# Dense layers of a graph network: last biases added by VectorE from a tile on all lanes, node rows stored chunk by chunk

## The chip, the cores and the metric

One core of one Trainium2 chip runs the kernel in one launch. The metric is the device time of that launch in microseconds (us), a median over runs; the profile is one more execution, recorded by the hardware profiler. PE is the matmul engine, PEld its weight loads, DVE VectorE, ACT ScalarE, POOL GpSimd, SP the engine whose queue issues most of the plain DMAs.

## The reference, cut to what matters

Four graph layers run one after the other on 6250 nodes of 32 features and 100,000 edges. Between the sums over edges, every node goes through small dense layers. Those that the change touches are:

```python
h = relu(h @ W1a + b1a);  h = relu(h @ W2a + b2a)     # 32 -> 64 -> 64, first half of layer 0 ("B" below)
h = relu(h @ W1b + b1b);  x = x + (h @ W2b + b2b)     # 64 -> 64 -> 32, second half ("C")
feat_src = h @ W2s + b2s; feat_dst = h @ W2d + b2d    # 32 -> 64 and 32 -> 64, layer 1 ("D")
x = x + ((feat + g_sum) @ W1 + b1)                    # 32 -> 32, end of layer 1 ("E")
t = elu(h @ stn3_w + stn3_b) @ stn4_w + stn4_b        # 64 -> 64 -> 3, layer 3 ("F")
```

A sixth product, 125 -> 64 without a bias ("A"), forms the first spline layer. The results of B (as three bf16 parts of each float, 192 values a node) and the source half of D (64 floats a node) are written to a table in device memory, `node_rows`, from which the next phase gathers a row for each edge.

## The kernel before, in words

The 6250 nodes lie as 49 blocks of 128: block j holds node 128 j + p on partition (lane) p. The program is a chain of phases. `phase` opens semaphores and buffers, the engines run their own instruction lists in it, and it ends with a clearing of its semaphores (line 78) and a barrier of all engines (L79), so nothing of a phase runs before the one ahead has ended.

`dense_phase` (L1076) makes all six products. It walks over 13 chunks: twelve of four blocks and a last one of one block. For a chunk, TensorE turns the blocks (L1142), ScalarE copies them out of PSUM (L1186), TensorE forms the hidden layer if there is one (L1157), ScalarE adds its bias and applies relu (L1198; for elu it is VectorE at L1219, L1220 and L1227 with ScalarE's exp at L1190), TensorE forms the last layer back in node order (L1168), and VectorE takes it out of PSUM with a `finish` function: `copy_to` (L1249), `over_zero_to` (L1270) or `add_to` (L1277). The stages are one chunk apart (`lags`): in one step, TensorE first makes the last layer of an older chunk, then the hidden layer of the next, then turns a third. Every PSUM and stage buffer is double; the semaphores `copied`, `made`, `back` and `taken` count chunks, and each engine waits for the counts in the order in which its list has them.

The last layer's bias lies in a tile of one partition, four times over. Before the products of L1168, TensorE multiplies a row of ones (cleared to 1.0 by VectorE at L1204) with it, which writes the bias to all 128 lanes of the PSUM bank (L1164); the products then add to it. This product stands behind the same waits (`copied`, `taken`) as the products of L1168.

Weights and biases are loaded by SP at the start of each dense phase, behind VectorE's clearing of the weight tiles (L1055, then L1062 for weights, L1068 for the last layer's bias and L1072 for a bias over partitions). The first product of a phase waits for all these loads.

In B, a `behind` function (L1260 to L1264) splits what was taken into three bf16 parts after each chunk. After B, and again after D, `store_nodes_phase` (L1028) writes the table in a phase of its own: one DMA of all 49 blocks (L1035), and a wait for it.

Of the kernel before, what the change touches and what calls it, by code (L numbers as in the profile page):

```python
# [7 lines left out]
BF16 = mybir.dt.bfloat16  # L8
# [1016 lines left out]

def store_nodes_phase(k, table, src):  # L1028
    nc = k.nc
    with phase(nc) as ph:  # L1030
        stored = ph.sem("stored")
        with nc.Block() as block:
            @block.sync
            def _(sp):
                sp.dma_start(table.rearrange("(j p) f -> p j f", p=LO), src).then_inc(stored, 16)  # L1035
                sp.wait_ge(stored, 16)


class Layer:


# [3 lines left out]
    def hold(self, k, ph, K, blocks, onwards):  # L1045


        self.K, self.blocks, self.onwards, self.ways = K, blocks, onwards, blocks // onwards
        self.weight = sb(k, ph, "weight", [blocks * K, self.ways, onwards * self.C])
        across_nodes = self.end is not None  # L1050
        self.bias = sb(k, ph, "bias", [onwards * self.C, 1] if across_nodes else [1, 4, self.C]) if self.biases else None
        self.loads = blocks * len(self.weights) + len(self.biases) * (onwards if across_nodes else 1)

    def clear(self, dve):
# [2 lines left out]
    def load(self, eng, sem):  # L1057
        for n in range(self.blocks):
            col = n % self.onwards * self.C
            for of in self.weights:  # L1060
                to = self.weight[n * self.K:(n + 1) * self.K, n // self.onwards, col:col + of.shape[1]]
                eng.dma_start(to, of).then_inc(sem, 16)  # L1062
                col += of.shape[1]
        col = 0
        for of in self.biases:
            width = of.shape[0]
            if self.end is None:
                eng.dma_start(self.bias[:, :, col:col + width], across(of, 4).unsqueeze(0)).then_inc(sem, 16)  # L1068
# [7 lines left out]
def dense_phase(k, src, K, layers, finish, behind=None):  # L1076

# [19 lines left out]
    with phase(nc) as ph:  # L1097
        for n, layer in enumerate(layers):
# [7 lines left out]
        ones = sb(k, ph, "ones", [1, LO])  # L1106
        turned, back, taken, own, cleared, weighed, ready = ph.sems("turned", "back", "taken", "own", "cleared", "weighed", "ready")
        copied = [ph.sem(f"copied{s}") for s in range(S + 1)]
        made = [ph.sem(f"made{s}") for s in range(S)]
        lowered = [ph.sem(f"lowered{s}") for s in range(S)]  # L1110
# [8 lines left out]
        with nc.Block() as block:  # L1119
            @block.sync  # L1120
            def _(sp):
                sp.wait_ge(cleared, S + 1)
                for layer in layers:
                    layer.load(sp, weighed)

            @block.tensor
            def _(pe):
                for step in range(len(chunks) + lags[-1]):
                    for s in range(S + 1, -1, -1):
# [30 lines left out]
                        else:  # L1160
                            if n >= 2:
                                pe.wait_ge(taken, n - 1)
                            if layer.bias is not None:
                                nc.tensor.matmul(out_p[b][:, 0:count, :].rearrange("p j f -> p (j f)"), ones[:],  # L1164
                                                 layer.bias[:, 0:count, :].rearrange("p j f -> p (j f)"), start=True, stop=False)
                            for q, blocks in stacks(S, count):
                                at = q // packs[S] * LO
                                m = nc.tensor.matmul(out_p[b][:, q:q + blocks, :].rearrange("p j f -> p (j f)"),  # L1168
                                                     of[0:blocks * layer.K, at:at + LO], layer.weight[0:blocks * layer.K, 0, 0:blocks * C_out],
                                                     start=layer.bias is None, stop=layer.bias is None or q + blocks == count)  # L1170
                            m.then_inc(back, 1)

            @block.scalar
# [27 lines left out]
            @block.vector  # L1201
            def _(dve):
                c = Chain(dve, own)
                dve.memset(ones[:], 1.0)  # L1204
                for layer in layers:
                    layer.clear(dve).then_inc(cleared, 1)

# [21 lines left out]
                for step in range(len(chunks) + 2):  # L1229
                    for s in range(1, S + 1):  # L1230
                        if elus[s - 1]:
                            if step < len(chunks):
                                raised(s, step)
                            if 0 <= step - 1 < len(chunks):
                                joined(s, step - 1)
                    n = step - 2
                    if n < 0:
                        continue
                    first, count = chunks[n]
                    dve.wait_ge(back, n + 1)  # L1240
                    finish(dve, out_p[n % 2][:, 0:count, :], first, count).then_inc(taken, 1)
                    if behind is not None:
                        dve.wait_ge(taken, n + 1)
                        behind(dve, c, first, count)


def copy_to(dest):
    def finish(dve, made, first, count):
        return dve.tensor_copy(dest[:, first:first + count, :], made)  # L1249
    return finish  # L1250


# [13 lines left out]


def over_zero_to(dest):
    def finish(dve, made, first, count):
        return dve.tensor_scalar(dest[:, first:first + count, :], made, 0.0, None, ALU.max)  # L1270
    return finish


def add_to(dest):
    def finish(dve, made, first, count):
# [1430 lines left out]
def gin_layers(k, s_rows, d_rows, making):  # L2706
    nc, w, n, xs = k.nc, k.w, k.dense_w, k.xs
    with layer(k):
        b = sb(k, None, "b", [LO, NB, D_HID])
        with layer(k):  # L2710
# [3 lines left out]
            with layer(k):  # L2714
# [6 lines left out]
                def keep(dve, c, ph):  # L2721
# [3 lines left out]
            first_sum_phase(k, d_rows, y)  # L2725
            add_phase(k, y, h)
            b16 = sb(k, None, "b16", [LO, NB, 3 * D_HID], BF16)
            dense_phase(k, y, D_IN, [Layer([n["W1a"]], [n["b1a"]], D_HID, "relu"), Layer([n["W2a"]], [n["b2a"]], D_HID)],
                        over_zero_to(b), split_to(k, b, D_HID, b16))
            table = dram(k, "node_rows", [NN, 3 * D_HID], BF16)  # L2730
            store_nodes_phase(k, table, b16[:])
        a = sb(k, None, "a", [LO, NB, D_HID])
        with layer(k):
            second_sum_phase(k, table, a, making)
# [5 lines left out]
def attention_layer(k, d_rows, lists, conv, shift):  # L2740
    n, xs = k.dense_w, k.xs
    with layer(k):
# [10 lines left out]
        with layer(k):  # L2753
            a.tops, a.sums = late("tops"), late("sums")
            with layer(k):
                feat = sb(k, None, "feat", [LO, NB, 2 * D_HID])
                dense_phase(k, h, D_IN, [Layer([n["W2s"], n["W2d"]], [n["b2s"], n["b2d"]], 2 * D_HID)], copy_to(feat))
                store_nodes_phase(k, table, feat[:, :, 0:D_HID])
# [130 lines left out]
```

## Time and profile before

| | |
|---|---|
| time, median of 3 runs | 11930.78 us (11922.58 to 11940.91) |
| profiled execution: span from first to last instruction | 11956.6 us |
| PE / DVE / POOL / ACT busy, share of the span | 49% / 53% / 52% / 28% |
| granted TensorE clock, mean of the span | 0.578 |
| dense phases with the stores behind them (A, B, C, D, E, F) | about 2871 to 2917, 3165 to 3234, 4808 to 4858, 4870 to 4945, 8420 to 8451, 8469 to 8525 us |

The profiled execution has no time of its own beside its span; the span is 25.8 us (0.2%) longer than the median of the three timed runs. In a timeline row the first two numbers are the start and the length in us, then engine, line, operation, output and input names, partitions and elements, and how many instructions the row merges; a bracket gives the idle time before it and what ended it. Names with digits are shown without them (`in_L_gnn_b2a_dram` is an input). A matrix product of 4-byte floats appears as two instructions.

### The profile page before, as it was taken

The page shows a single profiled execution, that of the slowest core. Times are in us where ns is not written, and L with a number is a line of the kernel's source. Part 1 is how long each engine was busy: PE and PEld are TensorE (multiplying, and loading weights), DVE is VectorE, ACT ScalarE, POOL GpSimd, SP SyncE. Part 2 cuts the span into 40 slices and gives each one's busy share as a digit, 9 for nine tenths or more (in the row PEclk, how much of TensorE's full clock was granted, in tenths as well). Part 3 has the DMA queues.
Part 4 walks back from the last instruction along what each step waited for, and adds up shares of the span by engine and source line. Part 5 has one row for each costly group of instructions (what it writes and reads, how often), then busy time and mean ns, then how long its engine had stood idle before and what let it go on. Part 6 is the DMA issues. An engine that isn't in the chain of part 4 may idle for free. (4 is left out here: it accounts for less than half of the span.)

```text
span 11956.6 us, 144077 instructions
## 1 busy us (share of the span) xinstructions
PE 5851.1 (49%) x32456; PEld 4649.4 (39%) x32585; DVE 6365.8 (53%) x16741; ACT 3375.5 (28%) x7561; POOL 6265.8 (52%) x8257
## 2 busy tenths in 40 slices
PE   4223244434566566566666466666433333742222
PEld 2111133333444344355555466666333333422222
DVE  6444555554311111366666788888455555654555
ACT  0000022222133333111111477777312111321111
POOL 3767566663155555255555344444055565046665
PEclk8555565655566666565656555555655555865555
DMA  6331222222555555122223699999111112876666
GB/s 192 111 110 57 60 56 58 58 57 66 169 190 190 183 190 175 34 67 67 67 66 66 262 350 349 350 350 351 73 38 38 38 38 37 296 256 199 194 199 180
DMA packets 894565, 1760.03 MB, mean 147 GB/s; under 512 B 486979, under 2 KB 487288, under 8 KB 889897
## 3 DMA queue, kind: packets, MB, share of 16 engines
q0 software_dynamic: 317952, 1023.05, 27.3%
q1 hardware_dynamic: 537384, 598.27, 15.0%
q10 hardware_dynamic: 39168, 138.04, 2.9%
q8 instruction: 23, 0.38, 0.0%
q14 instruction: 38, 0.30, 0.0%
HBM read 1150.36 MB, written 611.50 MB: 147 GB/s over the span
## 5 line engine op out<-in xcount | busy, mean ns | idle before, releaser
L1764 POOL DMA_INDIRECT got<-corners,now x1664 | 1599.6, 961 | 1835.4 <-issue 1064.2
L1764 POOL DMA_INDIRECT got<-node_rows,now x1664 | 1602.6, 963 | 1713.3 <-issue 1334.6
L1764 POOL DMA_INDIRECT got<-patches,now x832 | 795.8, 956 | 899.5 <-issue 603.1
L948 POOL DMA_INDIRECT d_rows<-row x832 | 836.0, 1005 | 533.7 <-issue 522.6
L1670 PE MATMUL made_p<-weights,turned 64*128 64x320 f32 x2450 | 795.4, 648 | 559.2 <-ACT z L1694 295.4
L2567 PE MATMUL sum_p<-msg_s,hot_s 128*128 128x64 f32 x3328 | 737.3, 423 | 595.4 <-DVE msg_s L2022 595.4
L699 POOL DMA_INDIRECT s_rows<-row_now,pos_i x784 | 756.6, 965 | 379.5 <-issue 372.0
L2567 PEld LDWEIGHTS sum_p<-msg_s,hot_s 128*128 128x128 f32 x3328 | 717.7, 332 | 604.3 <-DVE msg_s L2022 604.3
L2106 PE MATMUL acc_p<-msg,hot_s 128*128 128x32 f32 x1664 | 376.2, 402 | 1004.5 <-DVE msg L2030 785.1
L1812 DVE TENSOR_TENSOR a<-a,sum_p 128x64 f32 x832 | 183.5, 221 | 1244.0 <-remote 785.5
L1694 ACT COPY z<-made_p 128x384 f32<-128x384 f32 x1225 | 526.4, 489 | 973.0 <-DMA d_rows<-row 516.7
L1670 PEld LDWEIGHTS made_p<-weights,turned 64*128 64x128 f32 x2450 | 457.7, 262 | 830.5 <-ACT z L1694 407.8
L2106 PEld LDWEIGHTS acc_p<-msg,hot_s 128*128 128x128 f32 x1664 | 362.7, 330 | 1018.8 <-issue 1018.8
L155 POOL MEMSET spare<- 128x192 f32 x2472 | 694.1, 281 | 0.9
L268 DVE TENSOR_TENSOR hot<-column,lo_s 128x1024 bf16<-128x1024 bf16 x312 | 215.2, 690 | 673.9 <-DMA got<-node_rows,now 645.2
L2016 DVE TENSOR_TENSOR got<-got,weight 128x512 f32<-128x512 f32 x832 | 518.7, 684 | 58.3 <-PE sum_p L2567 19.5
L2092 ACT CAST hot_s<-hot 128x1024 f32<-128x1024 bf16 x104 | 212.4, 2042 | 1148.1 <-DVE hot L268 898.8
L886 DVE TENSOR_TENSOR sums<-sums,sum_p 128x126 f32 x832 | 237.9, 286 | 557.6 <-DMA d_rows<-empty 320.0
L2681 ACT ACTIVATE prod<-prod,below,alpha 128x32 f32<-128x32 f32 x1664 | 516.4, 398 | 0.0
L912 PE MATMUL feat_p<-h,turned_s 128*128 x832 | 122.1, 264 | 770.3 <-ACT turned_s L926 694.5
L632 PE MATMUL rank_p<-one,before 128*128 128x400 bf16 x98 | 48.8, 498 | 858.2 <-DVE one L417 697.2
L1961 ACT COPY turned_s<-turned_p 128x1024 bf16<-128x1024 bf16 x104 | 105.3, 1012 | 1265.1 <-remote 717.2
(424 smaller groups left out, 15148.1 us busy)
## 6 DMA issues: line engine op xcount, KB each, us to landing
corners<-z SPq DMA_DIRECT2D x245, 960.0 KB
corners<-z SPq DMA_DIRECT2D x98, 864.0 KB
d_rows<-empty ACTq DMA_DIRECT2D x32, 1586.0 KB
row<-d_rows SPq DMA_DIRECT2D x104, 488.0 KB
corners<-z SPq DMA_DIRECT2D x49, 672.0 KB
s_rows<-empty ACTq DMA_DIRECT2D x32, 962.0 KB
row<-s_rows SPq DMA_DIRECT2D x104, 296.0 KB
got<-node_rows,now POOLq DMA_INDIRECT x1664
```

What stands on the lines that cost most here:

```text
L155: pool.memset(self.of[:, t, :], 0.0).then_inc(self.cleared, 1)
L268: return dve.tensor_tensor(out, column16, mid(lo, LO), ALU.is_equal)
L699: pool.indirect_dma_start(out=s_rows, out_offset=bass.IndirectOffsetOnAxis(ap=pos_i[b][:, t, 0:1], axis=0), in_=row_now[b][:, t, :], in_of ...
L886: c.after(dve.tensor_tensor(to, to, part(1 - b2, t), ALU.add))
L948: pool.indirect_dma_start(out=d_rows, out_offset=bass.IndirectOffsetOnAxis(ap=to[:, t, DPOS:DPOS + 1], axis=0), in_=row[b][:, t, :], in_of ...
L1670: nc.tensor.matmul(self.made_p[s % self.BANKS][:, 0:self.col], self.turned[rows, :], self.weights[rows, q * self.col:(q + 1) * self.col], ...
L1694: self.k.nc.scalar.copy(to, of).then_inc(self.out, 1)
L1764: pool.indirect_dma_start(out=to[b][:, t, :], out_offset=None, in_=table, in_offset=bass.IndirectOffsetOnAxis(ap=indices.now[b][:, t:t + 1 ...
L2016: m = dve.tensor_tensor(v, v, last(weights[:, now, 2 * n:2 * n + 2], C), ALU.mult)
L2106: m = nc.tensor.matmul(at_block(acc, now[t]), hot_s[b2][:, t, :], msg[b2][:, t, :], start=False, stop=False)
L2567: m = nc.tensor.matmul(sum_p[b2][:, t, :], hot_s[b2][:, t, :], msg_s[b2][:, n, t, :], start=n == 0, stop=n == 1)
L2681: m = nc.scalar.activation(at[:, n, :], at[:, n, :], ACT.Exp, bias=below[b2][:, n:n + 1], scale=alpha[b2][:, n:n + 1])
```

## The change

The bias tile of a last layer becomes 128 partitions by C, loaded by SP from device memory with the same C values for every partition. TensorE's product with the ones is gone, and so are the ones and their clearing. The `finish` functions get the bias as an operand, repeated over the blocks of the chunk: `copy_to` adds instead of copying (a plain copy stays where there is no bias), `over_zero_to` adds out of PSUM and then takes the maximum with zero in SBUF, `add_to` adds the bias to the destination and then the product, in two instructions. VectorE waits for the loads once per phase and counts a few semaphores more per chunk. The store phases are gone: SP, behind its loads, waits for each chunk to be finished by VectorE and stores its rows, and waits for all stores at its end. Three more semaphores belong to each dense phase.

```diff
-def store_nodes_phase(k, table, src):
-                sp.dma_start(table.rearrange("(j p) f -> p j f", p=LO), src).then_inc(stored, 16)
-                sp.wait_ge(stored, 16)
...
-        self.bias = sb(k, ph, "bias", [onwards * self.C, 1] if across_nodes else [1, 4, self.C]) if self.biases else None
+        self.bias = sb(k, ph, "bias", [onwards * self.C, 1] if across_nodes else [LO, self.C]) if self.biases else None
...
-                eng.dma_start(self.bias[:, :, col:col + width], across(of, 4).unsqueeze(0)).then_inc(sem, 16)
+                eng.dma_start(self.bias[:, col:col + width], across(of)).then_inc(sem, 16)
...
+                if shelf is not None:
+                    table, of = shelf
+                    rows = table.rearrange("(j p) f -> p j f", p=LO)
+                    for n, (first, count) in enumerate(chunks):
+                        sp.wait_ge(shelved, n + 1)
+                        sp.sem_inc(storing, 1)
+                        sp.dma_start(rows[:, first:first + count, :], of[:, first:first + count, :]).then_inc(stored, 16)
+                    sp.wait_ge(stored, 16 * len(chunks))
...
-                            if layer.bias is not None:
-                                nc.tensor.matmul(out_p[b][:, 0:count, :].rearrange("p j f -> p (j f)"), ones[:],
-                                                 layer.bias[:, 0:count, :].rearrange("p j f -> p (j f)"), start=True, stop=False)
...
-                                                     start=layer.bias is None, stop=layer.bias is None or q + blocks == count)
+                                                     start=True, stop=True)
...
-                dve.memset(ones[:], 1.0)
...
+                    if n == 0:
+                        dve.wait_ge(weighed, held)
+                        dve.sem_inc(ready, 1)
                     dve.wait_ge(back, n + 1)
-                    finish(dve, out_p[n % 2][:, 0:count, :], first, count).then_inc(taken, 1)
+                    dve.sem_inc(ready, 1)
+                    added = None if bias is None else mid(bias[:], count)
+                    finish(dve, c, out_p[n % 2][:, 0:count, :], added, first, count).then_inc(taken, 1)
+                    if behind is not None or shelf is not None:
+                        dve.wait_ge(taken, n + 1)
+                        dve.sem_inc(ready, 1)
                     if behind is not None:
-                        dve.wait_ge(taken, n + 1)
                         behind(dve, c, first, count)
+                    if shelf is not None:
+                        dve.sem_inc(shelved, 1)
...
 def over_zero_to(dest):
+    def finish(dve, c, made, bias, first, count):
+        to = dest[:, first:first + count, :]
+        c.after(dve.tensor_tensor(to, made, bias, ALU.add))
+        return dve.tensor_scalar(to, to, 0.0, None, ALU.max)
...
 def add_to(dest):
+    def finish(dve, c, made, bias, first, count):
         to = dest[:, first:first + count, :]
+        c.after(dve.tensor_tensor(to, to, bias, ALU.add))
         return dve.tensor_tensor(to, to, made, ALU.add)
```

`c.after` lets VectorE wait until the instruction has finished.

## Rows read from the trace of the kernel before

**Rows 1.** Windows: bounds, us, busy of PE, PEld, DVE, ACT, POOL, clock, DMA, GB/s

```profile
2870.00:2917.00 47.00, 36.29 (x147) 32.32 (x147) 5.57 (x15) 7.30 (x13) 0.00 (x0) 0.50 0.01 1
4877.00:4935.00 58.00, 52.61 (x64) 15.58 (x64) 8.59 (x13) 3.18 (x12) 0.00 (x0) 0.50 0.00 0
3300.00:4800.00 1500.00, 936.78 (x4856) 606.60 (x4856) 264.95 (x1032) 518.01 (x1219) 861.34 (x1187) 0.67 0.54 184
```

**Rows 2.** Timeline of B: one step of the products, and the next one's begin

```profile
3211.61 1.22 PE L1164 MATMUL out_p<-bias,ones 1*128 1x256 f32 x2 [0.35 <-ACT stage L1198]
3212.75 1.22 PE L1168 MATMUL out_p<-weight,stage 128*128 128x128 f32 x4
...
3214.86 0.47 ACT L1198 ACTIVATE stage<-made_p,bias 128x256 f32<-128x256 f32 x1 [3.16 <-PE made_p L1157]
3215.39 1.22 PE L1164 MATMUL out_p<-bias,ones 1*128 1x256 f32 x2 [0.35 <-ACT stage L1198]
```

**Rows 3.** Timeline of B: VectorE's last two chunks, without a pause between them

```profile
3217.87 0.42 DVE L1270 TENSOR_SCALAR b<-out_p 128x256 f32<-128x256 f32 x1 [1.46 <-PE out_p L1168]
3218.33 0.29 DVE L1260 CAST b<-b 128x256 bf16<-128x256 f32 x1
3218.66 0.43 DVE L1261 TENSOR_TENSOR rest<-b,b 128x256 f32<-128x256 f32 x1
...
3220.23 0.23 DVE L1270 TENSOR_SCALAR b<-out_p 128x64 f32<-128x64 f32 x1
...
3221.47 0.19 DVE L1264 CAST b<-rest 128x64 bf16<-128x64 f32 x1
```

**Rows 4.** The store after B: timeline, and SP's waits (us in total, times, longest)

```profile
3222.62 0.40 SPq L1035 DMA_DIRECT2D node_rows<-b  x1
SPq L1032 <- DMA node_rows<-b: 10.3, 1, 10.3
3234.16 0.34 SPq L1626 DMA_DIRECT2D weights<-wide_w  x1
```

**Rows 5.** Timeline of C: the product with the ones and what follows it

```profile
4819.89 0.79 PE L1164 MATMUL out_p<-bias,ones 1*128 1x128 f32 x2
4820.61 0.69 PE L1168 MATMUL out_p<-weight,stage 128*128 128x64 f32 x2
```

**Rows 6.** Timeline of D: one chunk, and the next one's first product

```profile
4882.21 2.07 PE L1164 MATMUL out_p<-bias,ones 1*128 1x512 f32 x2 [0.36 <-ACT stage L1186]
4884.20 2.08 PE L1168 MATMUL out_p<-weight,stage 128*128 128x512 f32 x2
...
4886.85 1.21 PE L1164 MATMUL out_p<-bias,ones 1*128 1x512 f32 x1 [0.35 <-ACT stage L1186]
```

**Rows 7.** The store after D: timeline and SP's waits

```profile
4934.49 0.29 DVE L1249 COPY feat<-out_p 128x128 f32<-128x128 f32 x1 [1.08 <-PE out_p L1168]
SPq L1032 <- DMA node_rows<-feat: 8.4, 1, 8.4
4945.48 0.13 PEld L2324 LDWEIGHTS spread_p<-zero 128*128 128x128 bf16 x2 [11.32 <-issue]
```

**Rows 8.** Timeline of F: the product with the ones and what follows it

```profile
8484.22 0.60 PE L1164 MATMUL out_p<-bias,ones 1*128 1x12 f32 x2 [0.87 <-DVE stage L1227]
8484.75 0.59 PE L1168 MATMUL out_p<-weight,stage 128*128 128x6 f32 x2
```

**Rows 9.** Timeline: clearing, loads of biases (B's, then constants), a store of 106 partitions

```profile
8420.26 0.17 DVE L1204 MEMSET ones<- 1x128 f32 x1 [0.95 <-PEq L79]
...
3170.01 0.69 SPq L1068 DMA_DIRECT2D bias<-in_L_gnn_b2a_dram  x1
3171.98 0.55 PE L1157 MATMUL made_p<-stage,weight 128*128 128x128 f32 x1 [6.47 <-DMA bias<-in_L_gnn_b2a_dram]
...
0.76 0.43 SPq L305 DMA_DIRECT2D attn<-in_L_gnn_attn_dram  x1
...
11948.85 5.11 SPq L2862 DMA_DIRECT2D out_dram<-xs  x1
```

More of the change, by code:

```diff
@@ L1023, in _ @@
                 close_sums(k, acc_p, 7).then_inc(summed, 1)
-def store_nodes_phase(k, table, src):
[L1029 to L1034, printed above, removed]
-                sp.dma_start(table.rearrange("(j p) f -> p j f", p=LO), src).then_inc(stored, 16)
-                sp.wait_ge(stored, 16)
 class Layer:
@@ L1073, in load, with dense_phase @@
             col += width
-def dense_phase(k, src, K, layers, finish, behind=None):
+def dense_phase(k, src, K, layers, finish, behind=None, shelf=None):
     nc = k.nc
@@ L1105, in dense_phase @@
                 for s in range(S)]
-        ones = sb(k, ph, "ones", [1, LO])
         turned, back, taken, own, cleared, weighed, ready = ph.sems("turned", "back", "taken", "own", "cleared", "weighed", "ready")
+        shelved, stored, storing = ph.sems("shelved", "stored", "storing")
         copied = [ph.sem(f"copied{s}") for s in range(S + 1)]
@@ L1203, in _ @@
                 c = Chain(dve, own)
-                dve.memset(ones[:], 1.0)
+                bias = layers[S].bias
                 for layer in layers:
@@ L1239, in _ @@
                     first, count = chunks[n]
+                    if n == 0:
+                        dve.wait_ge(weighed, held)
+                        dve.sem_inc(ready, 1)
                     dve.wait_ge(back, n + 1)
-                    finish(dve, out_p[n % 2][:, 0:count, :], first, count).then_inc(taken, 1)
+                    dve.sem_inc(ready, 1)
[4 more added lines that the diff above has]
+                        dve.sem_inc(ready, 1)
                     if behind is not None:
-                        dve.wait_ge(taken, n + 1)
                         behind(dve, c, first, count)
+                    if shelf is not None:
+                        dve.sem_inc(shelved, 1)
 def copy_to(dest):
-    def finish(dve, made, first, count):
-        return dve.tensor_copy(dest[:, first:first + count, :], made)
+    def finish(dve, c, made, bias, first, count):
+        to = dest[:, first:first + count, :]
+        return dve.tensor_copy(to, made) if bias is None else dve.tensor_tensor(to, made, bias, ALU.add)
     return finish
@@ L1268, in over_zero_to, with finish @@
 def over_zero_to(dest):
-    def finish(dve, made, first, count):
-        return dve.tensor_scalar(dest[:, first:first + count, :], made, 0.0, None, ALU.max)
+    def finish(dve, c, made, bias, first, count):
+        to = dest[:, first:first + count, :]
+        c.after(dve.tensor_tensor(to, made, bias, ALU.add))
+        return dve.tensor_scalar(to, to, 0.0, None, ALU.max)
     return finish
 def add_to(dest):
-    def finish(dve, made, first, count):
+    def finish(dve, c, made, bias, first, count):
         to = dest[:, first:first + count, :]
+        c.after(dve.tensor_tensor(to, to, bias, ALU.add))
         return dve.tensor_tensor(to, to, made, ALU.add)
@@ L2727, in gin_layers @@
             b16 = sb(k, None, "b16", [LO, NB, 3 * D_HID], BF16)
+            table = dram(k, "node_rows", [NN, 3 * D_HID], BF16)
             dense_phase(k, y, D_IN, [Layer([n["W1a"]], [n["b1a"]], D_HID, "relu"), Layer([n["W2a"]], [n["b2a"]], D_HID)],
-                        over_zero_to(b), split_to(k, b, D_HID, b16))
-            table = dram(k, "node_rows", [NN, 3 * D_HID], BF16)
-            store_nodes_phase(k, table, b16[:])
+                        over_zero_to(b), split_to(k, b, D_HID, b16), (table, b16))
         a = sb(k, None, "a", [LO, NB, D_HID])
@@ L2756, in attention_layer @@
                 feat = sb(k, None, "feat", [LO, NB, 2 * D_HID])
-                dense_phase(k, h, D_IN, [Layer([n["W2s"], n["W2d"]], [n["b2s"], n["b2d"]], 2 * D_HID)], copy_to(feat))
-                store_nodes_phase(k, table, feat[:, :, 0:D_HID])
+                dense_phase(k, h, D_IN, [Layer([n["W2s"], n["W2d"]], [n["b2s"], n["b2d"]], 2 * D_HID)], copy_to(feat),
+                            shelf=(table, feat[:, :, 0:D_HID]))
                 score_phase(k, table, feat, d_rows, a)
```

## The prediction, made before the changed kernel was run

> **What bounds the kernel now.** No engine does: on the page's first part PE, DVE and POOL are each busy for about half of the span. The program is a chain of phases with a barrier behind each, so what counts is the length of each phase, and the change touches some 340 us of 11956.6. I therefore read busy time by windows first, then the timeline inside each dense phase, then SP's waits. The windows show two things [rows 1]: in D, TensorE is busy for 52.61 of 58.00 us while VectorE is at 8.59 and ScalarE at 3.18, so TensorE sets D; and the granted clock there is 0.50, that is 1.2 GHz, as it is in A.
>
> The timeline of B [rows 2] shows the circle that sets a step: the product with the ones starts only when ScalarE's relu (0.47 us) has ended, the last layer's products follow, then the hidden layer's, then relu again. 3215.39 - 3211.61 = 3.78 us a chunk, of which 3212.75 - 3211.61 = 1.14 us lie between the start of the product with the ones and the start of the real ones. That product stands behind the wait for relu, so it is on the circle and not beside it. VectorE has 1.46 us of idle time a chunk in B [rows 3], waiting for PE. After the dense work, DMA alone is at work: SP waits 10.3 us for B's store and 8.4 us for D's, and all other engines stand at the barrier [rows 4, 7].
>
> **The products with the ones.** I take the distance of starts, not the length, since consecutive instructions overlap at their ends. It counts for twelve full chunks and once less for the last one of a single block.
> - C: 4820.61 - 4819.89 = 0.72 us [rows 5]; the last chunk has 32 columns, between F's 12 and C's 128, so between 0.53 and 0.72, nearer to the first: 12 x 0.72 + 0.55 = 9.2.
> - D: 4884.20 - 4882.21 = 1.99 us [rows 6]; the last chunk has 128 columns, as C: 12 x 1.99 + 0.72 = 24.6. D's step is 4886.85 - 4882.21 = 4.64 us and becomes 2.65; VectorE's 13 copies take 8.59 us in all [rows 1], 0.66 each, and an add that reads one more operand, were it even twice as long, stays hidden under it.
> - E has the same product of 128 columns as C: 9.2 again.
> - F: 8484.75 - 8484.22 = 0.53 us [rows 8]; 13 x 0.53 = 6.9. Its circle is VectorE's elu, then PE, and an add of 12 elements replaces a copy of 12.
> - C and E have one more VectorE instruction a chunk. It is hidden (a two-operand instruction of 256 elements takes 0.43 [rows 3], these have 128) except in the last chunk, where it delays the end by about 0.2 us and a handover of 0.04 (below): -0.5 in all.
> - A has no bias and gains nothing here.
>
> In **B** the gain is not the whole 1.14 us, because VectorE takes over as the bound. Without the product, PE's circle is 3.78 - 1.14 = 2.64 us. VectorE's six instructions take 3220.23 - 3217.87 = 2.36 us when nothing holds them [rows 3]. The seventh is the maximum with zero in SBUF. No row has it; the nearest are the cast of 256 elements in SBUF (0.29) and the two-operand instruction (0.43). I take 0.29, since it too has one input, plus 0.04 for the handover that the rows show between two chained ones: 2.69. The three semaphore counts more a chunk have no row on VectorE; below, they cost nothing, above, 0.1 us each, more than twice a whole handover. I take 0.02 each: 2.75 us a chunk, between 2.69 and 3.13 (0.43 for the maximum, 0.1 for each count). Before, VectorE takes twelve full chunks in 11 x 3.78 + 2.36 = 43.9 us; after, in 12 x 2.75 = 33.0. Its first take comes 1.14 us earlier, and the last chunk's small seventh instruction and counts add 0.19 + 0.04 + 0.06: 43.9 - 33.0 + 1.14 - 0.29 = 11.8 us. With 3.13 a chunk it is 7.2.
>
> **The stores.** B's last VectorE instruction ends at 3221.66 and the next phase begins at 3234.16 [rows 3, 4]: 12.5 us of tail, made of 0.96 to the issue, 0.40 of issue, 10.3 of waiting and 0.84 of barrier. In the new kernel twelve of thirteen chunks are written while later ones are computed: 10.3 us for 49 blocks make 0.84 us for a chunk of four, and 0.40 to issue it, against a step of 2.75. What stays is the last store. The nearest row for a short DMA from issue to release is the bias load, 3171.98 - 3170.01 = 1.97 us [rows 9]. So the tail is 0.05 + 1.97 + 0.84 = 2.9 us, and the gain 9.6. D's tail is 4945.48 - 4934.78 = 10.7 us [rows 7]; 10.7 - 2.9 = 7.8 gained; a chunk there is 8.4 x 4/49 = 0.7 us of transfer under a step of 2.65. SP has nothing else queued behind its loads, so its new waits hold up no other transfer.
>
> The Trainium skill, "DMA: Bandwidth & Descriptors", sections "Anatomy of one DMA" and "Bandwidth", speaks against this part: each DMA has a fixed cost of about 2.0 us, most of it the receipt of the last write, and one should batch to 1 MiB, where a chunk here has 512 rows of 384 bytes, 192 KB. By its fit a chunk of B would take 2.0 + 0.45 us if no two overlapped, an estimate from that page, still under the step; the last one's 2.1 us would show, and the gain of the two tails would be 0.3 us less in sum. No run here shows a store of this size.
>
> **Small edits.** The clearing of the ones (0.17 us) goes from in front of the weights' clearing in six phases, and SP's loads and PE's start wait for that: 6 x 0.14 = 0.9. The six bias loads (two in D) go to 128 partitions. Issuing one took 0.69 in B; a load of the same kind, 64 floats to 128 partitions, took 0.43 [rows 9]. It moves 128 runs instead of four, so it may land later; I take zero in sum, with 0.26 us less and 0.3 more as bounds for each, so 1.8 us either way. VectorE's new wait for the loads is passed before PE's first product. Three more semaphores a phase are cleared behind the barrier; I put them at 0.2 us in all.
>
> **Sum**: 9.2 + 24.6 + 9.2 + 6.9 - 0.5 + 11.8 + 9.6 + 7.8 + 0.9 - 0.2 = 79.3 us. From the profiled span that is 11956.6 - 79.3 = 11877.3; the span is 25.8 us above the median of the timed runs, and the difference is carried over: 11930.8 - 79.3 = 11851.5, or 0.66% faster.
>
> **The rivals.**
> 1. *The products were hidden anyway.* If the distance of starts were weight loading or waiting that stays, only the stores and clearings gain: 9.6 + 7.8 + 0.9 - 0.2 = 18 us, 11913. For it: PE waits again and again. Against it: the waits end ahead of L1164, and L1168 follows it at once on the same engine.
> 2. *The clock opens in C, D, E and F.* The product with the ones has one row of 128 (1*128 in the rows); without it only full products are left in these stretches, and the clock might be granted in full. At 2.4 GHz, PE's parts of the remaining circles would halve: in D, all of its 2.65 but the 0.36 of idling [rows 6], so 1.15 a chunk. I take the same for C and F and half for E: 12 x 1.15 x 3.5 = 48 us more, 11803. Against it: A has only full products, is busy for 36.29 of 47.00 us, and stays at 0.50 [rows 1]. The Trainium skill, "TensorE: Matmul & The Clock Gate", section "Why this matters for your kernels", says to keep TensorE busy without a break to get past half rate. D before is busy nine tenths of 58 us and stays at half rate, so the trace does not agree in this place.
> 3. *SP's issue becomes the bound.* One store here, of 106 partitions, held SP's queue for 5.11 us [rows 9]. If each chunk store and each of the six bias loads did, B's 13 stores would take 66.4 us from its first finished chunk at about 3178, and the next phase begin at 3178 + 66.4 + 2.4 = 3246.8, 12.6 later than now; D's, from about 4880, 3.3 later; the loads would add 6 x (5.11 - 0.69) = 26.5. C, E and F with the clearings of four phases give 9.2 + 9.2 + 6.9 - 0.5 + 0.6 = 25.4. Sum: 17 us slower, 11948. Against it: loads and stores over 128 partitions were issued in 0.40 to 0.43.
> 4. *A lower clock in the stage behind B* (the other side). The sum over edges, 3300 to 4800 us, has 936.78 us of PE at a clock of 0.67 [rows 1]. B ends with less PE work, and the stage starts another way. At 0.50 its PE time would be 936.78 x 0.67/0.50 = 1255, 318 more; with half of it on the path, 159 - 79 = 80 slower, 12011. It decides once a quarter to a third of the 318 reaches the span. Against it: the stretches ahead of it are at 0.50 already, so it starts at the lower level now as well.
>
> **How the numbers follow.** Forecast 0.85, rival 1 0.04, rival 2 0.03, rival 3 0.02, rival 4 0.02, unnamed mixtures 0.04 (0.02 faster, 0.01 each same and slower). The median's own spread is 10 us either way. The unknown costs reach from 3 us more gain (loads 1.6, B 0.7, tails) to 9 less (4.6 in B, 1.8 in loads, 2 in tails). Added up that is 11838 to 11871; with some room for the sizes of the products' last chunks and towards rival 2, I give 11826 to 11880, and what lies outside is less than 2 in 10. A measurement tells a change from none at about 0.2%, 24 us. Faster 0.85 + 0.03 + 0.02 = 0.90, same 0.04 + 0.02 + 0.01 = 0.07, slower 0.02 + 0.01 = 0.03.
>
> **What would show it.** The step of a chunk shorter by 0.72 us in C and E, by 0.53 in F, and 2.65 in D; in B, VectorE without idle time at about 2.75 a chunk and PE waiting for `taken`. From VectorE's last instruction to the next phase: 2.9 us after B and D. The clock still 0.50. The forecast is wrong if B's or D's step stays above 3.2 us, if SP waits over 3 us for the last store, or if stages that the change does not touch differ by more than 10 us.

## The result, and the profile after

| | before | after |
|---|---|---|
| time, median of 6 runs each | 11916.21 us (11890.57 to 11940.91) | 11867.24 us (11859.49 to 11889.0) |
| profiled execution, span | 11956.6 us | 11887.2 us |
| granted TensorE clock, mean | 0.578 | 0.581 |

The ratio is 0.9966, with a 95% interval of 0.9951 to 0.9981: faster, as forecast, since the whole interval lies below 1; the kernel takes 11867.2 us where 11851.5 was said and 11826 to 11880 allowed. The medians differ by 49 us, the profiled spans by 69. What the change can touch is read more sharply from the dense stretches in the timelines, from the first product of each to the first instruction of the phase behind it (us):

| | A | B | C | D | E | F | B to F | all the rest |
|---|---|---|---|---|---|---|---|---|
| before | 46.05 | 69.06 | 49.96 | 74.88 | 31.22 | 56.41 | 281.5 | 11675.1 |
| after | 46.08 | 52.57 | 42.20 | 32.50 | 23.68 | 50.58 | 201.5 | 11685.7 |

They lost 80.0 us; the forecast had 79.3. That agreement is partly luck: D gained 10 us more than forecast, and B and the starts of the phases less. Windows of the changed kernel, in B twice, then in D, C, E and F (columns as in [rows 1]; the clock stands behind POOL):

```profile
3187.00:3197.00 10.00, 6.13 (x39) 4.80 (x38) 7.78 (x22) 3.15 (x10) 0.00 (x0) 0.90 0.22 60
3202.00:3216.00 14.00, 9.71 (x39) 7.55 (x38) 11.19 (x34) 2.87 (x9) 0.00 (x0) 0.50 0.24 66
4864.00:4884.00 20.00, 16.09 (x35) 5.41 (x35) 7.61 (x11) 2.93 (x11) 0.00 (x0) 0.89 0.31 66
4814.00:4840.00 26.00, 24.42 (x79) 17.47 (x78) 5.80 (x20) 7.81 (x20) 0.00 (x0) 0.50 0.00 0
8374.00:8386.00 12.00, 8.81 (x27) 5.40 (x27) 5.15 (x18) 2.39 (x9) 0.00 (x0) 0.50 0.01 1
8420.00:8450.00 30.00, 22.13 (x73) 16.03 (x72) 11.60 (x36) 7.11 (x18) 0.00 (x0) 0.50 0.00 1
```

In D the clock went from 0.50 to the full 2.4 GHz after the first chunks. The timeline of D shows a chunk every 1.59 us (4873.65 - 4872.06) where [rows 6] have 4.64 and the forecast 2.65; the first three chunks still stood 2.6 us apart, which is the forecast's step at its clock:

```profile
4872.06 1.12 PE L1162 MATMUL out_p<-weight,stage 128*128 128x512 f32 x2 [0.36 <-ACT stage L1180]
4873.02 0.27 PE L1139 MATMUL in_p<-ident,h 128*128 128x128 f32 x1
4873.33 0.69 DVE L1253 TENSOR_TENSOR feat<-out_p,bias 128x512 f32<-128x512 f32 x1 [0.90 <-PE out_p L1162]
4873.65 1.12 PE L1162 MATMUL out_p<-weight,stage 128*128 128x512 f32 x2 [0.35 <-ACT stage L1180]
```

In B VectorE sets the step, as forecast, but at 3205.62 - 3202.60 = 3.02 us. The timeline shows the gaps, 0.15 us from the maximum (L1276) to the cast (L1264) and 0.26 before the next add (L1275), where chained instructions without a count stand 0.03 to 0.04 apart. PE waits for L1276, that is for `taken`. One step early in B took 3.43 us; it is there in all four profiles in which VectorE adds the bias with all three counts and the rows are stored chunk by chunk, and its cause stays open:

```profile
3202.60 0.42 DVE L1275 TENSOR_TENSOR b<-out_p,bias 128x256 f32<-128x256 f32 x1 [0.26 <-DVE b L1268]
3203.06 0.29 DVE L1276 TENSOR_SCALAR b<-b 128x256 f32<-128x256 f32 x1
3203.50 0.29 DVE L1264 CAST b<-b 128x256 bf16<-128x256 f32 x1
...
3205.07 0.29 DVE L1268 CAST b<-rest 128x256 bf16<-128x256 f32 x1
...
3205.62 0.42 DVE L1275 TENSOR_TENSOR b<-out_p,bias 128x256 f32<-128x256 f32 x1 [0.26 <-DVE b L1268]
...
3206.52 1.20 PE L1162 MATMUL out_p<-weight,stage 128*128 128x128 f32 x4 [0.76 <-DVE b L1276]
```

The start of B, and its end. The last bias load ends its issue at 3177.84 and PE starts 3.07 us later; in [rows 9] it is 1.28. From VectorE's last instruction (3222.54) to the next phase it is 2.53 us, where [rows 3, 4] give 12.5:

```profile
3177.26 0.58 SPq L1057 DMA_DIRECT2D bias<-in_L_gnn_b2a_dram  x1
3180.91 1.19 PE L1154 MATMUL made_p<-stage,weight 128*128 128x128 f32 x4 [8.00 <-DMA bias<-in_L_gnn_b2a_dram]
...
3222.34 0.20 DVE L1268 CAST b<-rest 128x64 bf16<-128x64 f32 x1
3225.07 0.33 SPq L1633 DMA_DIRECT2D weights<-wide_w  x1
```

The same two rows at the start of D, 2.59 us between the end of the issue and PE:

```profile
4860.62 0.43 SPq L1057 DMA_DIRECT2D bias<-in_L_gnn_b2d_dram  x1
...
4863.64 2.05 PE L1162 MATMUL out_p<-weight,stage 128*128 128x512 f32 x2 [7.32 <-DMA bias<-in_L_gnn_b2d_dram]
```

### The profile page after: what moved, and what is told of

It is laid out like the page before. It is cut to its first block and busy times, and to the rows that moved or that the text cites. A ratio compares the mean times of both kernels' runs of the same rounds, so it can differ in the third digit from the quotient of the medians.

```text
span 11887.2 us, 143975 instructions
## 1 busy us (share of the span) xinstructions
PE 5759.6 (48%) x32326; PEld 4601.4 (39%) x32455; DVE 6368.5 (54%) x16774; ACT 3373.4 (28%) x7561; POOL 6278.5 (53%) x8257
```

## The experiments

Twelve more runs were made, two of them of the changed kernel again and one of the kernel before again. In question were the clock in D, the late start, and B's step. Dense stretches in us; "rest" is the span less B to F.

| kernel | median / before on the same chip | ratio, 95% interval | B | C | D | E | F | B to F | rest |
|---|---|---|---|---|---|---|---|---|---|
| e1_before | 11724.95 / 11729.6 | 1.0002, 0.9983 to 1.002 | 69.87 | 49.95 | 75.02 | 31.19 | 56.61 | 282.6 | 11466.4 |
| e1_after | 11632.58 / 11729.6 | 0.993, 0.991 to 0.9951 | 52.22 | 42.18 | 32.12 | 23.90 | 50.61 | 201.0 | 11420.0 |
| e1_bias_only | 11667.69 / 11729.6 | 0.995, 0.9929 to 0.9972 | 61.51 | 42.21 | 40.40 | 23.30 | 50.62 | 218.0 | 11463.1 |
| e1_stores_only | 11712.59 / 11729.6 | 0.9989, 0.9968 to 1.0011 | 59.56 | 49.99 | 66.80 | 31.32 | 56.41 | 264.1 | 11445.7 |
| e2_full_ones | 11866.18 / 11917.6 | 0.9955, 0.994 to 0.9971 | 53.32 | 46.90 | 51.37 | 28.11 | 55.26 | 235.0 | 11650.0 |
| e2_bias_first | 11843.66 / 11917.6 | 0.9944, 0.993 to 0.9957 | 50.41 | 40.49 | 31.16 | 22.18 | 49.22 | 193.5 | 11657.3 |
| e2_fewer_counts | 11846.76 / 11917.6 | 0.9943, 0.9927 to 0.9958 | 48.89 | 42.07 | 33.06 | 23.18 | 50.67 | 197.9 | 11682.5 |
| e2_both | 11837.3 / 11917.6 | 0.9934, 0.9921 to 0.9948 | 47.21 | 40.52 | 32.11 | 21.76 | 49.18 | 190.8 | 11644.5 |
| e3_ones_64 | 11728.78 (1 run) / 11712.13 | | 69.49 | 50.23 | 75.89 | 31.58 | 57.12 | 284.3 | 11442.7 |
| e3_mix | 11626.02 / 11712.13 | 0.9923, 0.9902 to 0.9943 | 45.29 | 40.59 | 30.02 | 21.81 | 49.19 | 186.9 | 11466.4 |
| e3_after | 11645.86 / 11712.13 | 0.9943, 0.9924 to 0.9962 | 52.60 | 42.16 | 34.09 | 23.89 | 50.56 | 203.3 | 11438.6 |

Each set had its own runs of the kernel before (11729.6, 11917.6 and 11712.13 us), and a median compares only with the one beside it. The twelfth, e4_full_rows, stands at the end.

### Where the time goes: the kernel before and after again

> The kernel before, unchanged, to have its trace and its time from the chip on which the other three run. Theory S (the six dense stretches with their stores carry the whole difference, and what else differs between the traces of before and after is the spread from chip to chip and run to run): its six stretches last the same 282 us as in the first trace, within 2 us in sum, whatever its span is. Rival O (the changed kernel also slows stages it does not touch, by 20 to 40 us): the rest of this trace, span less those stretches, is 20 us or more shorter than that of e1_after on the same chip.

> The changed kernel, unchanged. Theory S: its six stretches sum to 202 us again (80 less than before), the rest is as long as in e1_before within 10 us, and the median is 65 to 85 us below the kernel before. Rival O: the median is only 35 to 50 us below. Whether the clock in D is granted in full again (a chunk every 1.59 us) or is at 0.50 (2.65 us) is open; at 0.50 D is 11 to 13 us longer.

No edit. Against the first pair the stretches repeat within 1 us; the kernel after is 81.6 us shorter in them here, 80.0 there. The rest, code that no edit touches, went 46 us down here and 10.6 up there. Theory S held for the stretches and missed twice: the rests differ by more than its 10 us, and the medians differ by 97 us, not 65 to 85. Rival O falls, since the rest is not longer in the changed kernel. So the verdicts below go by the stretches, and the medians stand beside them.

### The two parts alone

```diff
# e1_bias_only: the changed kernel with the stores in phases of their own again
-    ... split_to(k, b, D_HID, b16), (table, b16))
+    ... split_to(k, b, D_HID, b16)); store_nodes_phase(k, table, b16[:])
# e1_stores_only: the kernel before with the chunk stores, and the product with the ones kept
+    sp.wait_ge(shelved, n + 1) ... sp.dma_start(rows[:, first:first + count, :], ...)
```

> VectorE adds the biases as in the changed kernel, but the rows are stored in a phase of their own as before. Theory S: stores as before add 17 us against the changed kernel (9.6 after B, 7.8 after D), so 62 us faster than before. If it is the missing product with the ones that lets the clock rise in D, D's chunks come every 1.59 us here too; if it is the stores beside the products, D is at 0.50 and 2.65 us. Rival O: if the chunk stores are what slows the later gathers, this kernel has no such loss and is as fast as the changed one or faster.

> Rows are stored chunk by chunk, but TensorE still makes the product with the ones. Theory S: 17 us faster than before, all of it in the tails of B and D (12.5 and 10.7 us become about 2.9); B and D's chunks still come every 3.78 and 4.64 us at a clock of 0.50. Rival O (chunk stores slow what follows): within 10 us of before or slower. If the clock rises in D here, it is not the product with the ones that kept it down.

The two parts touch different times and nearly add: 64.6 us (282.6 - 218.0) and 18.5 (282.6 - 264.1), 83.1 against 81.6 together. The stores' 9.6 + 7.8 of the forecast is confirmed by the stretches (B -10.3, D -8.2); the median alone would not show it, as its interval holds 1. The middle of D, in windows of the one and then of the other kernel, shows which part the clock goes with:

```profile
4808.00:4823.00 15.00, 11.80 (x30) 3.99 (x28) 6.22 (x9) 2.40 (x9) 0.00 (x0) 0.99 0.00 1
```

```profile
4782.00:4797.00 15.00, 13.94 (x17) 3.68 (x15) 2.08 (x3) 0.80 (x3) 0.00 (x0) 0.50 0.15 32
```

Without the product with the ones TensorE is less busy (11.80 of 15 us against 13.94) and gets twice the clock. These two windows stand at different clocks. At the same clock, 0.50, D of the changed kernel from its first product to the rise, and then D of the kernel before, where no rise comes:

```profile
4863.64:4868.37 4.73, 4.38 (x6) 1.43 (x6) 0.69 (x1) 0.27 (x1) 0.00 (x0) 0.50 0.13 28
4887.00:4900.00 13.00, 12.29 (x15) 3.53 (x15) 1.39 (x3) 0.53 (x2) 0.00 (x0) 0.50 0.00 0
```

TensorE was busy for 93% of the one and 95% of the other, so its busy share is not what tells them apart.

### What about that product held the clock

```diff
# e2_full_ones: the kernel before, the product 128 rows deep (rows beyond the first are zero)
-        self.bias = ... [1, 4, self.C]) if self.biases else None
+        self.bias = ... [LO, 4, self.C]) if self.biases else None      # cleared, the bias loaded into row 0
-        ones = sb(k, ph, "ones", [1, LO])
+        ones = sb(k, ph, "ones", [LO, LO])
# e3_ones_64: the same with 64 rows
```

> The kernel before, but the product with the ones in all dense phases is 128 rows by 128 columns of weights instead of 1 by 128: a bias tile of 128 lanes whose first lane holds the bias and whose others hold zero, and ones of 128 by 128. The numbers computed, the products, their order, columns and waits are as before; only the rows that each of them uses change. One more clearing a phase. Theory R (the one-row product kept the clock at half in D): now D holds only full products, the clock in D rises after a few chunks as in the changed kernel, and a chunk there takes about 2.5 us instead of 4.64 (1.99 + 2.29 halved, plus the 0.36 of idling), so D falls from 75 us by 15 to 25 us; the whole is about 20 us faster than before. Rival W (it is the waiting, since the changed kernel waits longer or in other places, or the removed work as such): D keeps 0.50 and 4.64 us a chunk, D stays at 75 us and the whole is the same or a few us slower by the clearings.

> The kernel before, with the product with the ones 64 rows deep instead of 1, the rows beyond the first zero; the same numbers computed. With 128 rows two things came together: at the same clock (0.50) the products behind it began 0.29 us sooner (C's step 3.07 us instead of 3.36, E's 1.79 instead of 2.08), and in B and D the clock rose to full. Theory T (the 0.29 us is the price of a change between products of one row and of 128, and any number of rows short of 128 pays it, as it may also hold the clock): C's step 3.36, E's 2.08. Rival U (it is the number of rows itself, the more the better): 64 rows stand between, or with the 128: C's step 3.07 to 3.2. Whether the clock of B and D is 0.50 or full then tells whether the clock goes with the same thing or apart from it; I expect that it rises in D (chunk about 2.5 us) with chance 0.5.

A product with 127 rows of zeros added made the kernel 0.45% faster (0.9955). Theory R holds for D, which lost 23.5 us where 15 to 25 were expected. The whole gained more than its 20: 46.5 us in the stretches, since B lost 15.7 and C, E and F together 7.3, of which the theory had said nothing. Windows of e2_full_ones, middle of B, D and C, then B from its first product to the rise of the clock; and the middle of D in e3_ones_64:

```profile
3176.00:3196.00 20.00, 15.90 (x105) 13.21 (x103) 18.25 (x52) 5.66 (x18) 0.00 (x0) 1.00 0.00 1
4875.00:4895.00 20.00, 17.16 (x41) 6.67 (x40) 5.54 (x8) 2.13 (x8) 0.00 (x0) 0.99 0.00 0
4815.00:4835.00 20.00, 19.17 (x68) 14.95 (x68) 2.02 (x7) 4.79 (x12) 0.00 (x0) 0.50 0.00 0
3168.79:3172.31 3.52, 3.17 (x11) 2.59 (x12) 0.00 (x0) 0.63 (x2) 0.00 (x0) 0.50 0.00 0
```

```profile
4827.00:4847.00 20.00, 18.58 (x23) 5.65 (x23) 2.77 (x4) 1.07 (x4) 0.00 (x0) 0.50 0.00 0
```

B and D have the full clock, C has not. D's chunk takes 2.45 us, B's 2.36, where VectorE's six instructions follow each other without idle time. C gained all the same, at half clock. Its timeline here, and that of e3_ones_64:

```profile
4826.96 0.80 PE L1164 MATMUL out_p<-bias,ones 128*128 128x128 f32 x2
4827.34 0.97 PEld L1168 LDWEIGHTS out_p<-weight,stage 128*128 128x128 f32 x4
4827.55 0.95 PE L1168 MATMUL out_p<-weight,stage 128*128 128x64 f32 x4
4828.30 1.17 PE L1157 MATMUL made_p<-stage,weight 128*128 128x256 f32 x2
...
4830.03 0.80 PE L1164 MATMUL out_p<-bias,ones 128*128 128x128 f32 x2
```

```profile
4772.38 0.79 PE L1164 MATMUL out_p<-bias,ones 64*128 64x128 f32 x2
4773.10 0.93 PEld L1168 LDWEIGHTS out_p<-weight,stage 128*128 128x128 f32 x4 [0.22 <-issue]
4773.10 1.11 PE L1168 MATMUL out_p<-weight,stage 128*128 128x64 f32 x4
4774.00 1.17 PE L1157 MATMUL made_p<-stage,weight 128*128 128x256 f32 x2
...
4775.73 0.79 PE L1164 MATMUL out_p<-bias,ones 64*128 64x128 f32 x2
```

With 128 rows the next weight load starts 0.38 us after the product with the ones has begun, beside it, and the step is 3.07 us. With 64 rows it starts 0.72 us after, and the step is 3.35, within 0.01 of the 3.36 with one row; all stretches are within 1.1 us of those of the kernel before, and the clock is 0.50 in B and D. So theory T holds and U falls, and my even chance that D's clock would rise with 64 rows went to the other side: in C and E a product of 1 or of 64 rows between full ones costs 0.29 us a chunk more at half clock than one of 128. In F, where it has 12 columns, the step was 3.90 us with 1 or 64 rows and 3.80 with 128, so the price is 0.10 there and not one number. Row counts between 64 and 128 were not run. The Trainium skill, "TensorEngine Tiling (Array Packing)", section "Key Properties", says that changing the tiling mode drains TensorE, and 64 and 32 rows are modes of their own there. The step of 3.35 us at 64 rows and 3.07 at 128 agrees; that a product of one row counts as such a mode, and the drain itself, no run shows.

Of the 0.72 us a chunk that C gained, then, 0.29 is this change of shape and 0.43 the product itself.

### The late start, B's counts, and both

```diff
# e2_bias_first: the last layer's bias loads go to the head of SP's list
+                layers[S].load_last_bias(sp, weighed)
                 sp.wait_ge(cleared, S + 1)
                 for layer in layers:
                     layer.load(sp, weighed)
# e2_fewer_counts
                     dve.wait_ge(back, n + 1)
-                    dve.sem_inc(ready, 1)
...
                         dve.wait_ge(taken, n + 1)
-                        dve.sem_inc(ready, 1)
```

> The changed kernel, but SP issues the load of the last layer's bias first, before it waits for the clearing of the weight tiles and before the weights' own loads. Theory L (a load of the same 64 floats to each of 128 lanes lands 1 to 2 us later than one to a single lane, and it is the last that the first product waits for): from the end of the last issue to the first product it is 1.3 us again, not 2.3 to 3.0, in B, C, D, E and F, and in sum the dense stretches are 5 to 8 us shorter than in the changed kernel (201 us become about 195). Rival Q (the wait is that of the whole queue, which writes into more lanes, whatever the order; or the loads ahead of it now end last): the distance stays above 2 us, and the sum within 1 us of 201.

> The changed kernel without two of VectorE's semaphore counts a chunk, the one behind its wait for the product and the one behind its wait for its own result. Theory N (each count costs VectorE about 0.11 us between two instructions: 0.26 and 0.15 us of gap where chained instructions have 0.04): B's chunk takes 2.8 us instead of 3.03, and B is 2.5 to 3 us shorter. Rival G (the gaps come from the waits for the result, which stay): 3.03 us and B unchanged. Other stretches within 1 us in either case.

> The changed kernel with both edits: the last layer's bias loaded first, and two counts fewer a chunk. If theories L and N hold they add, since one is at the start of each phase and the other in each chunk of B: 201 us of dense stretches become 190 to 193, about 9 us (0.08%) less than the changed kernel and about 90 less than before, which the median alone can hardly tell and the stretches can. If they don't add, B's gap moves to the wait for relu, at 2.64 us a chunk or more.

Theory L holds: the stretches lose 8.0 us. The first product that needs the loads comes 8.6 us earlier, summed over the five phases: 5.8 of that is the shorter wait behind the last issue, and the rest is the issue of the bias load, which now runs beside the clearing. In B of e2_bias_first the last load is one of weights, and PE starts 3160.26 - 3158.72 = 1.54 us after its issue:

```profile
3157.48 1.24 SPq L1057 DMA_DIRECT2D weight<-in_L_gnn_W2a_dram  x2
3160.26 1.19 PE L1159 MATMUL made_p<-stage,weight 128*128 128x128 f32 x4 [5.86 <-DMA weight<-in_L_gnn_W2a_dram]
```

Theory N holds as well. In B of e2_fewer_counts the step is 3186.95 - 3184.14 = 2.81 us, and the cast follows the maximum by 0.04:

```profile
3184.14 0.42 DVE L1273 TENSOR_TENSOR b<-out_p,bias 128x256 f32<-128x256 f32 x1
3184.60 0.30 DVE L1274 TENSOR_SCALAR b<-b 128x256 f32<-128x256 f32 x1
3184.93 0.29 DVE L1262 CAST b<-b 128x256 bf16<-128x256 f32 x1
...
3186.95 0.42 DVE L1273 TENSOR_TENSOR b<-out_p,bias 128x256 f32<-128x256 f32 x1
```

So two counts cost 0.22 us a chunk. B as a whole is 3.7 us shorter, more than the 2.5 to 3 expected: the counts give 2.6, and the rest is an earlier start and the absence of the one long step. In e2_both the gains nearly add: 201.5 - 190.8 = 10.7 us, where 8.0 and 3.6 were gained singly.

### A version from these results

```diff
# e3_mix: e2_both, but in B the bias comes from a product again, with ones of 128 rows
-  Layer([n["W2a"]], [n["b2a"]], D_HID)
+  Layer([n["W2a"]], [n["b2a"]], D_HID, product=True)
```

> A version put together from what the runs gave: the changed kernel with the last bias loaded first and two counts fewer, but in B the bias comes from a product with ones of 128 rows again, so that VectorE has six instructions a chunk there and TensorE only full products. Expected: in B TensorE's clock is full and VectorE sets the step at 2.36 us instead of about 2.8; B lasts 42 to 44 us instead of 47, the other stretches as before it (C 40.5, D 31 to 32, E 22, F 49), the sum 185 to 188. Rival: B's clock falls back to half when VectorE holds TensorE up, the step stays above 2.6 us, and B is 46 us or more.

> The changed kernel as it is, beside the version above on the same chip, so that the two can be compared: dense stretches 201 to 202 us in sum, D at full clock again (1.59 us a chunk) and C, E and F at 0.50. The version above should be 13 to 16 us shorter in the stretches, and 0.1% in the medians if their spread allows it. Theory that the clock in D came by chance: it would be 0.50 in some of the runs of this kernel, and D 43 us; so far it was full in each.

B's clock is full and stays so until TensorE's last product there (first row). In B of e2_both, where VectorE adds the bias and TensorE comes to wait for it, the clock was full for 17 us (second row) and then back at 0.50:

```profile
3126.00:3146.00 20.00, 15.49 (x101) 12.69 (x99) 17.41 (x50) 6.14 (x20) 0.00 (x0) 1.00 0.26 69
3161.00:3177.00 16.00, 8.91 (x67) 7.36 (x66) 13.96 (x41) 4.42 (x14) 0.00 (x0) 1.00 0.28 74
```

```profile
3133.03 0.42 DVE L1293 TENSOR_SCALAR b<-out_p 128x256 f32<-128x256 f32 x1
3135.06 0.29 DVE L1285 CAST b<-rest 128x256 bf16<-128x256 f32 x1
3135.51 0.42 DVE L1293 TENSOR_SCALAR b<-out_p 128x256 f32<-128x256 f32 x1
```

The step is 2.48 us, not 2.36: the count `shelved`, which the stores need, costs 0.12; in e1_bias_only, without it, B's step was 2.94 against 3.03, so 0.09. B takes 45.29, between expectation and rival; the rival's cause (a clock that falls back) is not what happened. Against e2_both it gains 1.9 us, though its first product comes 1.3 us later, since the bias load waits again for a cleared tile. The stretches are 16.4 us below e3_after. The medians are 20 us apart, but the intervals overlap, so the runs alone don't prove it the faster of the two; both beat the kernel before. In e3_after D's clock was full again, but after four steps and not two, and D took 34.09.

### Are full rows enough?

```diff
# e4_full_rows: e3_mix, and in A products of 128 rows (3 rows of weights zero) instead of 125
-  dense_phase(k, sums[:, :, 0:K3], K3, ...)
+  dense_phase(k, sums, LO, ...)                 # sums is 128 wide
```

> The version put together before, and in A, which no version so far has touched, products of 128 rows and columns instead of 125: the tile of sums is 128 wide, the three more rows of its weights are zero, so the same numbers are computed, the products have the same moving columns and the same order. Theory T (a product short of 128 rows or columns keeps the clock of a stretch at half that would else be granted in full): A, at 0.50 and 46 us in every run so far, rises to full after the first chunks; its products' part halves, about 1.3 us of each 3.4 us chunk, and A lasts 28 to 36 us. Rival V (what counts is only that the product with the ones is nearly empty or that it changes the shape between two products; A has pauses for ScalarE and is busy 77% of its time, less than D's 90%): A stays at 0.50 and 46 us. The other stretches within 2 us of the version before (B 45.3, C 40.6, D 30, E 21.8, F 49.2).

```profile
2830.00:2850.00 20.00, 15.95 (x69) 13.54 (x69) 2.55 (x6) 3.52 (x6) 0.00 (x0) 0.50 0.00 0
```

Theory T falls in this form: A took 44.92 us, 1.1 less, at 0.50 as ever. The median was 11641.0 against 11704.34 (0.9934, 0.9914 to 0.9953), not to be told from e3_mix. The other stretches were to stay within 2 us of e3_mix; D missed that with 33.22 us, since its clock rose only after four steps, and B to F took 191.5. So short products kept the clock of B and D down, but full ones don't raise it in A, C, E or F. TensorE's busy share doesn't sort them either: in e2_full_ones it was busy for 19.17 of 20 us in C, and the clock stayed at 0.50; in B it was busy for 3.17 of the 3.52 us at 0.50 behind which the clock rose. What else is wanted stays open, and so does how soon D's clock rises: it took one to four steps, and D's stretch was 30.02 us in e3_mix and 33.22 here, with the same code in D.

## Why the prediction was right, and where it was not

The direction and the range held, and 79.3 us of forecast met 80.0 in the stretches, by errors that cancelled. Step by step, with times from the timelines of the two kernels:

- **C, E, F.** From VectorE's first take of a chunk to its last: C 39.23 to 30.64 us, E 24.57 to 16.08, F 41.03 to 34.86, so 8.6, 8.5 and 6.2 less. Twelve times the distances of starts [rows 5, 8] are 8.6, 8.6 and 6.4. Right, and for the reason given: the product stood on the circle that sets the step. The distance contained the change of shape, which I had not known as a part of its own.
- **D.** 52.81 to 19.68 us, 33.1 less where 12 x 1.99 = 23.9 was forecast. The sentence that failed is "The clock still 0.50"; while it was 0.50, the first chunks came every 2.61 us, as the forecast's 2.65. Rival 2, given 0.03 as a whole, came true in D alone (and for some 10 us of B, where it won nothing, as VectorE sets the step). Its price was nearly right (1.15 us a chunk; 2.65 - 1.59 = 1.06 measured), its place was not: it named C, E and F too. The argument against it was that A "has only full products"; A's are of 125 rows, and though e4_full_rows shows that this is not what holds A, A was no evidence on D.
- **B.** 44.09 to 36.72, 7.4 less; 10.9 were forecast (43.9 - 33.0). VectorE does bound it, and the maximum takes the 0.29 I took. The term mis-sized is the semaphore count: 0.02 us assumed, 0.11 measured, three a chunk. The bound of 0.1 each was nearly the value; I called it "more than twice a whole handover" and went for the other end without a row that was near.
- **The stores.** Tails of 2.53 us (B) and 2.60 (D) where 2.9 was forecast, 18.1 gained against 17.4. Rival 3 didn't happen. The estimate from the Trainium skill beside the forecast, 2.1 us for a last store, rests on a section about DMAs that GpSimd issues, which I had not said; here SP issues them. From the issue of B's last store at 3222.68 to the next phase at 3225.07 it took 2.4 us, barrier included.
- **Bias loads and clearings.** This term was wrong by the most against its bounds. From a phase's start to the first product that needs the loads: B 6.88 to 8.41 us, C 6.17 to 7.26, D 6.99 to 7.74, E 4.18 to 5.38, F 6.03 to 6.88, in sum 5.4 later, where the clearings should have made it 0.7 earlier. I bounded the six loads at 0.3 us each from their issue times. The issue did become cheaper (0.58 for 0.69 in B), but from the end of the last issue to the first product it is 1.1 to 1.8 us more than with the load to one lane, and e2_bias_first shows that it is this load and its place in the queue. Why it lands later was not tested.
- **The rest of the program** differs by 10.6 us between the two profiles, just over the 10 that I had set as a sign of failure. e1_bias_only and e1_after, alike there, differ by 43 us in it, so the threshold was too tight. Rival 4 finds nothing: from B's end to C it was 1574.4 us before and 1576.5 after. The three measurements of the change, 0.9966, 0.993 and 0.9943, are 49, 97 and 66 us by their medians, about the 80 of the stretches; the first lies below it with its whole interval (23 to 58 us), the intervals of the other two hold it. Whether a few us are given back elsewhere can't be told. The 15.7 us between forecast and median are not explained by any step of the sum, and they are luck in part: the forecast was counted from 11930.8, the median of three runs, and from the 11916.2 of six it would have been 11836.9, 30.3 us below what was measured.

Together: 79.3 - 3.5 (B) - 6.1 (starts) + 9.2 (D's clock) + 0.7 (stores) = 79.6, against 80.0 measured.

## What to carry to other kernels

A product with few rows between full ones can cost more than its columns: here a change of shape, 0.10 to 0.29 us a chunk, and in two of five stretches the clock. Take it off TensorE, or, where the next engine has no room for the work, fill it up to 128 rows with zeros; in B that beat moving it by 1.9 us. When a load goes from one lane to many, put it ahead of the others in the queue, and count the semaphore instructions of an engine that becomes the bound.

## What the runs showed of the hardware

- D reached 2.4 GHz in ten profiles out of ten without the short product, after one to four chunks, and stayed at 1.2 GHz in four out of four with it (1 or 64 rows). The Trainium skill, "TensorE: Matmul & The Clock Gate", section "Why this matters for your kernels", ties the clock to keeping TensorE busy without a break; D was busy for 12.29 of 13.00 us with the short product and stayed at half clock, and for 4.38 of 4.73 without it and rose, so the trace does not agree in this place.
- A product of 1 or 64 rows between products of 128, against one of 128 rows: 0.29 us a chunk more in C and E, 0.10 in F, at half clock. In A, 128 rows for 125 gave 0.10 (3.60 to 3.50 us).
- A semaphore count on VectorE between two chained instructions: 0.09 to 0.12 us.
- A load of 64 floats to each of 128 lanes: 3.07 us in B and 2.59 in D from the end of its issue to the product that waits, against 1.28 in B for one lane.
- Twelve chunk stores beside the work left the steps as they were: 3.79 us in B and 4.64 in D in e1_stores_only, 1.59 in D with and without them. Only VectorE's count for each store (0.09 to 0.12 us) and the one step of 3.43 us in B stand against them.
